# Splitting the issue of a key exchange, another form of the shift, and three steps moved

## The reference

```python
x = x + xattn(layernorm(x), ctx)   # 16 heads of 64; keys and values from ctx: 16 x 1024 x 256
x = x + attn(layernorm(x))         # linear attention with a feature map, 16 heads of 16
x = x + ffn(layernorm(x))          # 8 experts, the best 2 of each row
```

```python
ctx = layer_norm(context, g, b);  q = lat @ Wq;  k, v = split(ctx @ Wkv)
k = apply_rope(k, cos, sin)        # [x1*cos - x2*sin, x2*cos + x1*sin]
p = softmax(clip(q @ k.T * scale, -11, 11));  out = (p @ v) @ Wo + bo
```

## Time and profile before

| | us |
|---|---|
| median of 3 runs | 1367.38 |
| lowest, highest | 1366.13, 1373.22 |
| the profiled execution | 1373.17 |
| its span, first to last instruction | 1371.4 |
| busy: PE, DVE, ACT, POOL | 1231.1, 1156.1, 653.0, 605.3 |
| mean granted clock of PE | 0.954 of full speed |

### The profile page before, as it was taken

How to read it: one execution, slowest core, us unless ns; L and a number is a source line. 1 busy time by engine, 2 the same in 40 slices (tenths; PEclk the granted TensorE clock), 3 DMA queues, 4 the chain that set the end, 5 groups by cost and what they waited for, 6 DMA issues and landing times.

```text
span 1371.4 us, 39825 instructions
## 1 busy us (share of the span) xinstructions
PE 1231.1 (90%) x16268; PEld 1036.8 (76%) x16268; DVE 1156.1 (84%) x1954; ACT 653.0 (48%) x1089; POOL 605.3 (44%) x611
## 2 busy tenths in 40 slices
PE   7888898988988989888898888988999999999997
PEld 3677777777767767767777777777778888789997
DVE  6799989998989998999889898888986736757886
ACT  7454444444444444444444444444544423346664
POOL 2455544454544444554444454444444313332333
PEclk9999999999999999999889898999999999999999
DMA  5365555555555555555456554555456371366662
GB/s 208 82 151 129 126 125 129 131 120 121 120 121 121 124 128 124 132 131 129 122 123 126 120 122 119 124 126 119 121 146 134 90 223 64 102 189 203 190 191 82
DMA packets 136173, 181.36 MB, mean 132 GB/s; under 512 B 30316, under 2 KB 96312, under 8 KB 135864
## 3 DMA queue, kind: packets, MB, share of 16 engines
q1 hardware_dynamic: 110552, 150.80, 43.4%
q10 hardware_dynamic: 21360, 23.80, 6.8%
q0 software_dynamic: 4080, 4.22, 1.5%
HBM read 81.93 MB, written 30.56 MB: 82 GB/s over the span
## 4 chain that ended last, share of the span: by engine, by line
DVE 49%; PE 39%; issue 7%; ACT 2%; DMA 2%; POOL 1%; SPq 0%; POOLq 0%; DVEq 0%; ACTq 0%
PE bank L1575 9%; DVE shift L1060 9%; DVE p_lo L1102 7%; PE bank L1561 7%; DVE kw L1114 6%; PE bank L1930 5%; DVE kr L1115 5%; DVE pr L1082 5%; DVE qo L1096 5%; PE bank L1627 4%; PE bank L1604 3%; DVE ct L1124 2%; DVE xt L1077 2%; DVE bst L1068 2%; DVE kr_fourth L1115 2%
## 5 line engine op out<-in xcount | busy, mean ns | idle before, releaser
L1575 PE MATMUL bank<-ct,wk_hi 128*128 128x512 f32 x1024 | 335.0, 409 | 5.9 <-DVE kr_third L1115 2.9
L1604 PE MATMUL bank<-p_hi,xc 128*128 128x512 f32 x1024 | 316.1, 390 | 0.0
L1575 PEld LDWEIGHTS bank<-ct,wk_hi 128*128 128x128 f32 x1024 | 190.0, 193 | 55.7 <-DVE kr L1115 8.7
L1114 DVE TENSOR_TENSOR kw<-bank,stab 128x512 f32<-128x512 f32 x256 | 175.3, 685 | 60.8 <-PE bank L1575 58.2
L1604 PEld LDWEIGHTS bank<-p_hi,xc 128*128 128x128 f32 x1024 | 191.9, 188 | 39.8
L593 POOL TENSOR_TENSOR kr<-kr,ksw 128x1024 f32<-128x1024 f32 x64 | 153.7, 2403 | 123.4 <-issue 120.5
L778 ACT CAST p_hi<-pr 128x1024 fp32r<-128x1024 f32 x128 | 134.3, 1049 | 150.4 <-DVE pr L1082 150.4
L1575 PE MATMUL bank<-ct,wk_lo 128*128 128x512 f32 x512 | 202.9, 396 | 0.0
L1604 PE MATMUL bank<-p_lo,xc 128*128 128x512 f32 x512 | 199.2, 389 | 0.0
L773 ACT ACTIVATE pr<-bank 128x1024 f32<-128x1024 f32 x128 | 127.8, 1026 | 81.6 <-PE bank L1561 81.5
L1060 DVE SCALAR_TENSOR_TENSOR shift<-mv,rstd 128x1 f32<-128x1 f32 x120 | 162.5, 1354 | 0.0
(11 more groups left out here) (227 smaller groups left out, 2190.8 us busy)
## 6 DMA issues: line engine op xcount, KB each, us to landing
ksw<-kw SPq DMA_DIRECT2D x512, 128.0 KB, 2.3
x_turned<-xt SPq DMA_DIRECT2D x120, 128.0 KB, 2.5
ct_read<-x_turned SPq DMA_DIRECT2D x30, 512.0 KB, 4.9
w_two<-in_L_ffn_W_dram SPq DMA_DIRECT2D x15, 1024.0 KB
raw<-in_ctx_dram ACTq DMA_DIRECT2D x56, 256.0 KB, 3.4
x_slots<-fill ACTq DMA_DIRECT2D x32, 258.0 KB, 3.3
w_all<-in_L_ffn_W_dram SPq DMA_DIRECT2D x4, 2048.0 KB, 17.0
wo<-in_L_ffn_W_dram SPq DMA_DIRECT2D x7, 1024.0 KB, 5.0
```

The lines of the kernel that those rows point to most:

```text
L1114: dve.tensor_tensor(by_tile(kw[:, i, cols]), keys_, by_tile(stab[:, places]), ALU.mult).then_inc(kw_done, 1)
L1575: last = pe.matmul(psK[:, a * 512:(a + 1) * 512], l[:, k, w], ct[:, h % 3, r, k], start=(m == 0), stop=(m == len(parts) - 1))
L1604: last = pe.matmul(psZ[c], xc[:, slot_, l, t, cols], r[:, i, :, t], start=(f == 0 and m == 0), stop=(f == 1 and m == len(parts) - 1), skip ...
```

## The change

There are four edits. (1) The exchange of `kw` for steps from 0 on: SP issues the first two of the four DMAs, and ScalarE the other two, in a new function `exchanged(j)` with the same two waits, called right behind `rows_high(j)` in every step; for the steps before 0 SP still issues all four. (2) The shift is made by `tensor_scalar` of the mean with `rstd` as a per-partition scalar and -1, in place of `scalar_tensor_tensor` with the mean and `rstd` as two tensors. (3) `divided` moves from behind `blocks_turned(j)` to ahead of `weights_low(j)`, next to the clamp of step j + 1. (4) On POOL the key sums of steps -2 and -1 move ahead of `deviations` and `rows_low` of their steps; those of the steps before, which do nothing, are gone.

```diff
--- before.py
+++ after.py
@@ -443,7 +443,7 @@
 
                     sp.wait_ge(kw_done, 2 * (j + 5))
                     wait(sp, kr_done, j + 3)
-                    for r in range(4):
+                    for r in range(4 if j < 0 else 2):
                         to, of = r * HALF, (r ^ 1) * HALF
                         sp.dma_start(ksw[to:to + HALF, i], kw[of:of + HALF, i]).then_inc(sw_ld[i], 16)
                 if due(j, 7):
@@ -627,10 +627,15 @@
                 pool.wait_ge(rstd_done, (2 * c + 1) * ST // 2)
                 pool.tensor_tensor(xl_rsd[:, t], xl_vpe[:, t], consts[:, 2:3].to_broadcast([P, ST // 2]), ALU.pow).then_inc(rstd_done, ST // 2)
             constants()
-            for j in range(-5, 0):
+            for j in range(-5, -2):
                 deviations(j)
                 rows_low(j)
-                keys_summed(j)
+            keys_summed(-2)
+            deviations(-2)
+            rows_low(-2)
+            keys_summed(-1)
+            deviations(-1)
+            rows_low(-1)
             for j in range(STEPS):
                 keys_summed(j)
                 deviations(j)
@@ -776,6 +781,15 @@
             def weights_high(j):
                 act.wait_ge(clamp_done, j + 1)
                 act.copy(step_part(p_hi, j), step_part(pr, j)).then_inc(p_hi_done, 1)
+
+            def exchanged(j):
+                if there(j + 4):
+                    i = j % 2
+                    act.wait_ge(kw_done, 2 * (j + 5))
+                    act.wait_ge(kr_done, j + 3)
+                    for r in range(2, 4):
+                        to, of = r * HALF, (r ^ 1) * HALF
+                        act.dma_start(ksw[to:to + HALF, i], kw[of:of + HALF, i]).then_inc(sw_ld[i], 16)
 
             def even_step(j):
                 if due(j, 6):
@@ -794,6 +808,7 @@
                     weights_high(j)
                 normalised(j)
                 rows_high(j)
+                exchanged(j)
                 if half_written(j - 1):
                     half_high(half_written(j - 1))
                 loads(j)
@@ -1057,8 +1073,7 @@
                     dve.wait_ge(rstd_done, 2 * (n + 1))
                     if n >= ST + 2:
                         dve.wait_ge(xhat_done, n - 1)
-                    dve.scalar_tensor_tensor(out=shift[:, i:i + 1], in0=mv[:, i, 0:1], scalar=-1.0, in1=rstd[:, i:i + 1],
-                                             op0=ALU.mult, op1=ALU.mult).then_inc(shift_done, 1)
+                    dve.tensor_scalar(shift[:, i:i + 1], mv[:, i, 0:1], rstd[:, i:i + 1], -1.0, ALU.mult, ALU.mult).then_inc(shift_done, 1)
 
             def counted(j):
                 for n in stats_at(j):
@@ -1133,10 +1148,10 @@
                 keys_turned(j, 0)
                 keys_turned(j, 1)
                 clamped(j + 1)
+                if due(j, 10):
+                    divided((j - 10) // 4)
                 weights_low(j)
                 blocks_turned(j)
-                if due(j, 10):
-                    divided((j - 10) // 4)
                 if due(j + 1, 7):
                     inverted((j - 6) // 4)
                 shifts(j + 1)
```

## The result

The changed kernel takes **1248.46 us**, the median of four runs (1245.46 to 1250.60). The kernel before, run beside it, took 1367.43 (1366.13 to 1373.22). The ratio is **0.912, interval 0.909 to 0.915**. The forecast was 1234 us. The profiled execution took 1248.36 us, and its span is 1246.6.

What follows compares the result with a forecast made beforehand. VectorE, held by GpSimd key sums, makes TensorE wait: 33.05 us quads fall to 28.3. 1373.2 − 128 (27 quads) − 9 (start) = 1236, less 2 gives 1234 us; likeliest range 1205 to 1268, 8-in-10 range 1205 to 1330.

Steps and rivals of the forecast that it cites:

- What bounds the kernel: Steady quads: GpSimd key sums hold VectorE, so TensorE waits before `outputs`; 33.05 us a quad against 27.2 without waits.
- The shift, unheld at 0.14 us: VectorE's new one-tensor, pointer-form shift is not held by a key sum: 0.14 us, against 2.3 if held.
- Even step, 0.5 us gained and 1.5 only moved: Behind the even step's shift the clamp is held until the key sum ends: 0.5 us gained, 1.5 only moved.
- Rival (1): Hold moves to clamps, `p_lo` and rounding; TensorE still idles before `outputs`: quads 30 to 31.5 us, around 1300; chance 0.19.
- rival (2): Pointer-form shift is held like the old one; nothing gained in the steady part: 1385 us, slower; chance 0.12.
- The division at 0.4 in the open: Division between second clamp and `p_lo` meets no key sum: 0.4 us instead of 2.5.
- VectorE's slack before `outputs`, 1.3 us: VectorE's last `kr` is ready 1.3 us before TensorE asks for it at `outputs`, so its work barely fits.
- The quad, 28.3: Steady quad: TensorE's 27.2 us, plus 0.5 for an issue stall in the scores, plus 0.6 for used-up slack.
- The exchange at nothing: ScalarE issuing half the exchange, 1.2 us more per step, is hidden and costs nothing; otherwise up to 1 us a quad.
- The key sums, 5 us: At the start, moving the first key sums up removes the second scores' 4.63 us wait and a slow stretch: 5 us.
- The further 4 us for two slow two-steps at the start: Two-steps before the first `outputs` last 19.0 and 17.3 us against 13.1 to 13.6 needed; 4 us taken as saved.
- The tail, nothing: After 1016 us only a little shift work is left, so nothing is gained there.

Runs made afterwards that it cites:

- short_sum: Kernel before with GpSimd's key sum cut to 64 of 1024 columns, nothing on VectorE changed: 1224.8 us.
- forms: Changed kernel with one small extra VectorE instruction behind the odd step's transposition, its form changing among five from one pair of steps to the next: 1307.03 us.
- u_shift: Changed kernel with the old two-tensor form of the shift, all else as changed: 1370.85 us, ratio 1.0056 to the kernel before.
- s_shift: Kernel before with the new form of the shift alone: 1288.27 us, ratio 0.942 to the kernel before.
- u_exch: Changed kernel with all four exchange DMAs issued by SP again, none by ScalarE: 1229.58 us, ratio 0.905 to the kernel before.
- thin_exch: Changed kernel with the exchange of steps from 0 on cut to 64 of 1024 columns, issued half and half as before: 1246.55 us, ratio 0.912.
- loads_first: Changed kernel with ScalarE's context load ahead of the exchange in odd steps instead of behind it: 1246.72 us, ratio 0.914.
- act4: Changed kernel with all four exchange DMAs issued by ScalarE, none by SP, in steps from 0 on: 1271.25 us, ratio 0.931.
- u_div: Changed kernel with the division back behind the transposition (`blocks_turned`): 1295.41 us, ratio 0.953 to the kernel before.
- u_keys: Changed kernel with GpSimd's key sums of steps -2 and -1 behind the statistics again: 1253.21 us, ratio 0.921 to the kernel before.
- split_x: Changed kernel with SP issuing all exchange DMAs, `scores(j + 1)` behind `keys(j + 4)`, and the second exponential behind `weights_high(j)`: 1237.89 us, ratio 0.905.

## Why the prediction was right, and where it was off

The direction, the main mechanism and, within 15 us, the size came out as forecast: 1248.5 against 1234, inside the likeliest case's own range of 1205 to 1268. (By the sum's own terms, 96 us and 3 us saved and 2 taken off, the upper end should read 1272; nothing hangs on it.) By the forecast's own sum the profiled execution should have taken 1236; the steady part cost 14.3 more (27 × 0.53), the start 3 less, the tail 1.3 more: 1248.6, against 1248.4.

- **What bounds the kernel.** Right. short_sum shows that the key sum is the holder and that the hold sets the pace. The quad without statistics as measure of TensorE's own time was right to the hundredth: undisturbed quads of the changed kernel last 27.20 us.
- **The shift, unheld at 0.14 us.** Right in size (0.175), and the choice between the two ends was the decision of the whole forecast. The reason was right in part only. I argued from one input tensor and a pointer, and forms shows that a pointer form of two elements is held. That the new shift came out free was in part luck: it has one element. The pointer rows that I took as free overlapped with only one short GpSimd instruction; the counter-evidence in the same group (0.31 instead of 0.19) was the truer sign. Why the 256-element forms of that group were not held by a GpSimd instruction of 1.01 us, while the two elements of forms are by a key sum, no run asks. The Trainium skill ("VectorE: DVE Perf Modes", Mode 2×_2P) says that a `tensor_scalar` between SBUF tensors may use both ports when its outermost non-unit dimension is even, or odd and equal. For two elements forms agrees, immediate or pointer. One element I had read as odd and equal, although the sentence speaks of a non-unit dimension, and 107, 110 and 175 ns beside a running sum speak against my reading; the Trainium skill says it more plainly in "Advanced Engine Details and Errata", Mode Summary, where an odd dimension must be above 1, and the three measurements agree. The Trainium skill ("SBUF — State Buffer", Who interferes with whom) says that a VectorE instruction with two SBUF inputs contends with a GpSimd instruction that reads SBUF, and the one-element `TENSOR_TENSOR` (2256 ns) agrees.
- **Even step, 0.5 us gained and 1.5 only moved.** Right for one step in four: the clamp at 617.31 takes 2.17 and stands until the sum ends, and clamps of that kind have a mean of 2.06 us (0.89 before). In the quad's other even step the clamp comes later and is held for less (1.07 against 0.72). Rival (1) thus took place in part; 77 of the 198 us freed moved to clamps and `p_lo`, and the slack that VectorE had won carried them. In u_shift the mechanism of rival (2) is to be seen, at less than its price: 1.0056, where 1385 us would have been 1.013.
- **The division at 0.4 in the open.** Right (0.412). What the prediction says of the shift in the odd step (that the division took its block) is half of a point that it doesn't draw out: the two edits need each other. The runs give 80 us to the shift alone (s_shift) and 128 to the shift on top of the three other edits (u_shift against the changed kernel). Without the shift those three leave the quads at 33.02 us; the move alone was not run.
- **VectorE's slack before `outputs`, 1.3 us.** Too large: in the changed kernel's quads with statistics the last `kr` ends 0.37 us before `outputs` starts. Of that only about 0.2 is slack, since the distance is 0.15 in the kernel before, where `outputs` does wait. One term left out is the 29 us of `p_lo` held by `xc`, some 0.2 us a step, two steps of which lie ahead of each `kr` in question. It comes in part from ScalarE's issues: in u_exch the distance is 0.66, and `p_lo` gains only 11 us. Some slack was left, so it cost nothing, but forms shows how soon it is used up.
- **The quad, 28.3.** It came to 28.83. The floor was right; the term for stalls was mis-sized. I put in 0.5 a quad from 14.0 us in 13 waits, as if a shorter kernel kept the same stalls, and 0.6 for used-up slack. Measured are 1.08 for stalls (29.3 / 27) and 0.54 for the rest, of which an estimated 0.4 is the clock that drops behind them. Even with SP issuing everything the stalls are longer than before (22.8 us in u_exch against 14.7, scores and keys together). They are 26.3 us in s_shift and 21.2 in short_sum, so they grew wherever the hold went; why was not tried.
- **The exchange at nothing.** Wrong, by 10 us in the ratios; it is the one term whose mechanism failed. I followed ScalarE's queue to `o_part` and the exponentials, and there it cost nothing. In the changed kernel the cost appears as longer stalls of TensorE's own instruction issue, nearly all at places that it had already, and as the lower clock behind them. Taking away the bytes (thin_exch), the load behind it (loads_first) or the second issuing queue (act4) does not give the time back. In kernels that TensorE sets the pace of, the stalls grow with the number of issues that ScalarE makes (22.8, 31.3, 39.2 us); in u_div and s_shift, where VectorE still does, they don't. Why stays open.
- **The key sums, 5 us.** Right: 5.2 us by u_keys. The further 4 us for two slow two-steps at the start came out at about 7 (12.1 less 5.2), since those two-steps are of the same kind as the quads; s_shift has 5.7 of it with the shift alone.
- **The tail, nothing.** 1.3 us lost, not followed up.

## What to carry to other kernels

When a VectorE instruction takes the rest of a GpSimd instruction's time whatever its size, ask not only how to free it but what stands behind it: the hold passes to the next instruction that can be held, and here the time was won where the instructions behind read PSUM, which a key sum does not hold. A price for "the same work without the wait" is best read from a stretch of the same trace in which the wait is missing; here it was right to 0.01 us. And once TensorE is the last, its own small stalls count in full: put them into the sum at no less than their present length, here 14 us, and they may grow (here to 31).

## What was not expected of the hardware

- A one-element instruction with one input is not held by a running key sum (medians of 0.11 to 0.18 us), the same with two elements is (2.27 to 2.29). Pointer forms of 256 elements took 0.41 us, no less than the two-tensor division of the same size when nothing holds it, and yet six of them held up a short GpSimd instruction. So the speed of a form doesn't tell whether it gets in GpSimd's way.
- What look like TensorE's instruction fetches are to be seen in the DMA records: 16 KB each, 0.9 to 1.8 us long in the changed kernel. In its rows of 192 short matmuls 18 of them are followed by a stall of 1.1 to 2.2 us (up to 5.0 in other runs). With long matmuls between (split_x) the issue waits of scores and keys are down to 1.6 us in all.
- ScalarE as issuer of the same transfers lengthened these stalls: 22.8, 31.3, 39.2 us for none, two and four of four.
- Putting 64 short matmuls among long ones costs TensorE 0.44 to 0.48 us each time (split_x), though it waits for nothing.
